# Issuing the loads of edges on ScalarE's queue in a sort-and-reduce graph kernel

## The reference

```
row = edge_index[0]                                     # src, unsorted, 400000 values below 12500
seg_sum = segment_sum(edge_attr, row, N)
seg_max = where(cnt > 0, segment_max(edge_attr, row, N), 0.0)
seg_mean = seg_sum / maximum(cnt, 1.0)
h = concatenate([seg_sum, seg_max, seg_mean, u[batch]], axis=1)
h = relu(h @ W1 + b1)
return x + (h @ W2 + b2)
```

## Time and profile before

| | us |
|---|---|
| median of 3 runs | 4303.77 (4302.16 to 4304.75) |
| the profiled execution, its own time | 4299.8 |
| its span, first to last instruction | 4298.0 |
| Pool busy | 3084.1 (72%), 3143 instructions |
| DVE busy | 2986.4 (69%) |
| PE busy | 2953.8 (69%) |
| ACT busy | 1418.7 (33%) |

### The profile page before, as it was taken

One profiled execution on the slowest core, in us unless ns is written; L12 is line 12 of the kernel. 1 busy time (PEld: TensorE's weight loads), 2 busy tenths in 40 slices (PEclk: granted clock), 3 DMA queues, 4 the chain that ended last, 5 costly groups with the idle time before them and its releaser, 6 DMA issues.

```text
span 4298.0 us, 87474 instructions
## 1 busy us (share of the span) xinstructions
PE 2953.8 (69%) x18710; PEld 2191.8 (51%) x18710; DVE 2986.4 (69%) x12043; ACT 1418.7 (33%) x4649; POOL 3084.1 (72%) x3143
## 2 busy tenths in 40 slices
PE   5677667776666666666666677777787777767747
PEld 3455446654444444444444466666665556546635
DVE  6478559974555455554455589988897888769976
ACT  3333332243333333333333323332233333322224
POOL 5777777777777777777777777776677777777620
PEclk9977558765555555555555578877776788668867
DMA  7899863311111111111111333333322333134333
GB/s 295 333 378 377 333 243 114 115 25 25 26 26 26 26 25 26 26 26 26 25 26 26 82 103 101 106 108 103 100 65 78 91 88 92 52 90 120 88 111 103
DMA packets 410044, 454.47 MB, mean 106 GB/s; under 512 B 65002, under 2 KB 381460, under 8 KB 409620
## 3 DMA queue, kind: packets, MB, share of 16 engines
q1 hardware_dynamic: 309876, 401.37, 28.4%
q0 software_dynamic: 100000, 51.40, 4.9%
HBM read 221.50 MB, written 231.02 MB: 105 GB/s over the span
## 4 chain that ended last, share of the span: by engine, by line
POOL 41%; issue 21%; DVE 20%; PE 7%; DMA 6%; POOLq 2%; DVEq 1%; ACT 1%; SPq 0%; ACTq 0%
POOL sorted_rows L439 41%; DVE peak_ps L799 5%; DMA sorted_rows<-edges,position 3%; DVE raised L782 3%; DVE picked L723 3%; PE misc_ps L526 3%; DMA edges<-in_edge_attr 2%; DVE lent L715 2%; PE start_ps L495 1%; DVE hot_owner L706 1%; POOLq L439 1%; DVE rank_c L733 1%; DVE peak_ps L777 1%; PE same_ps L472 1%; DVE raised L810 1%
## 5 line engine op out<-in xcount | busy, mean ns | idle before, releaser
L439 POOL DMA_INDIRECT sorted_rows<-edges,position x3125 | 3075.2, 984 | 1035.5 <-issue 927.7
L499 PE MATMUL place_ps<-start_sb,lent 98*128 98x128 bf16 x3125 | 877.7, 281 | 1019.2 <-DVE rank_f L723 1017.6
L610 ACT ACTIVATE start_sb<-start_ps 98x128 bf16<-98x128 f32 x3125 | 867.6, 278 | 1660.1 <-PE start_ps L495 806.0
L495 PE MATMUL start_ps<-hot_owner,hot_block 128*98 128x128 bf16 x3125 | 980.1, 314 | 143.9 <-ACT start_sb L610 105.5
L723 DVE CUSTOM_DVE_ANT_0 picked<-place_ps,hot_owner 128x128 bf16<-128x128 f32 x3125 | 886.2, 284 | 102.0 <-issue 61.5
L499 PEld LDWEIGHTS place_ps<-start_sb,lent 98*128 98x128 bf16 x3125 | 377.6, 121 | 1131.2 <-DVE rank_f L723 1100.1
L501 PE MATMUL place_ps<-hot_owner,lent 128*128 128x128 bf16 x3125 | 894.8, 286 | 0.0
L738 DVE SCALAR_TENSOR_TENSOR position<-rank_c,src_f 128x5 int32<-128x5 f32 x625 | 104.4, 167 | 1057.2 <-DMA sorted_rows<-edges,position 1007.2
L495 PEld LDWEIGHTS start_ps<-hot_owner,hot_block 128*98 128x98 bf16 x3125 | 460.6, 147 | 625.6 <-ACT start_sb L610 614.6
L472 PE MATMUL same_ps<-lent 98*128 98x128 bf16 x3125 | 654.2, 288 | 74.9 <-DVE lent L715 35.3
L526 PE MATMUL misc_ps<-win,ident_f 128*128 128x224 f32 x2548 | 699.6, 437 | 0.0
(11 more groups left out here) (79 smaller groups left out, 1402.3 us busy)
## 6 DMA issues: line engine op xcount, KB each, us to landing
sorted_rows<-zeros SPq DMA_DIRECT2D x110, 1568.0 KB, 17.1
win<-sorted_rows SPq DMA_DIRECT2D x56, 1344.0 KB
edges<-in_edge_attr SPq DMA_DIRECT2D x625, 80.0 KB
sorted_rows<-edges,position POOLq DMA_INDIRECT x3125
win<-sorted_rows SPq DMA_DIRECT2D x28, 1008.0 KB
win<-sorted_rows SPq DMA_DIRECT2D x14, 1680.0 KB
win<-sorted_rows SPq DMA_DIRECT2D x14, 1568.0 KB
win<-sorted_rows SPq DMA_DIRECT2D x14, 896.0 KB
```

Of the source, the lines that this page charges most:

```text
L439: nc.gpsimd.indirect_dma_start(out=rows[:, :], out_offset=bass.IndirectOffsetOnAxis(ap=position[:, t:t + 1], axis=0), in_=edges[:, k, j * ...
L495: nc.tensor.matmul(start_ps[0:BLOCKS, 0:P], hot_block[:, t, :], hot_owner[:, t, :], start=False, stop=False, skip_group_check=True).then_i ...
L499: nc.tensor.matmul(place_slot(j), hot_block_t[:, slot, j * P:(j + 1) * P], start_sb[:, j, :], start=True, stop=False)
L610: nc.scalar.activation(start_sb[:, j, :], start_ps[0:BLOCKS, 0:P], ACT.Copy)\
```

## The change

SP keeps its wait for the sent group but issues no load; in the load's place it increments a semaphore for which nobody waits. ACT issues the load at the end of the step in which it has copied the counts of the same group, behind the second copy of the transposed blocks. Ahead of the load ACT waits for the same `edges_sent` as SP and DVE, except for the first five groups.

```diff
--- before.py
+++ after.py
@@ -309,10 +309,6 @@
                 sp.dma_start(rows[bass.ds(plane * PLANE, PLANE), :].rearrange("(p k b) f -> p k (b f)", p=P, k=2),
                              zeros[:, :].unsqueeze(1).to_broadcast([P, 2, FILL])).then_inc(done, 16)
 
-            def load_group(c, at, k):
-                sp.dma_start(edges[:, k, :], edge_view[:, bass.ds((at * CHUNK + k * GROUP) * FEAT, GROUP * FEAT)])\
-                    .then_inc(edges_loaded[k], 16)
-
             def load_half(s, f, r, h):
                 plane = BASE[s] + r
                 part = rows[plane * PLANE:(plane + depth[s]) * PLANE, :]
@@ -348,7 +344,7 @@
                     for k in range(GROUPS):
                         if n != 0:
                             sp.wait_ge(edges_sent[k], c * (16 * GROUP))
-                        load_group(c, at, k)
+                        sp.sem_inc(pass_seen, 1)
                         if done is not None:
                             fill(at * FILLS + (BASE[1] - FILLS + k), done)
                             if k == GROUPS - 1:
@@ -622,6 +618,16 @@
                     if has(n, LAG_TRANSPOSE):
                         nc.scalar.activation(hot_block_t[:, slot, 2 * P:], hot_t_ps[0:BLOCKS, 2 * P:GROUP * P], ACT.Copy)\
                             .then_inc(hot_copied, 1)
+                    if has(n, LAG_PLACE):
+                        k = (g - LAG_PLACE) % GROUPS
+                        load_group(c - 1 if g < LAG_PLACE else c, at - 1 if g < LAG_PLACE else at, k,
+                                   n is not None and n < LAG_PLACE + GROUPS)
+
+                def load_group(c, at, k, begin):
+                    if not begin:
+                        act.wait_ge(edges_sent[k], c * (16 * GROUP))
+                    act.dma_start(edges[:, k, :], edge_view[:, bass.ds((at * CHUNK + k * GROUP) * FEAT, GROUP * FEAT)])\
+                        .then_inc(edges_loaded[k], 16)
 
                 def chunk(c, at, n, s, pair):
                     for g in range(GROUPS):
```

## The result

| | before | after |
|---|---|---|
| median of the timed runs, us | 4303.68 (4300.32 to 4311.19) | 4314.36 (4307.51 to 4325.16) |
| ratio to before, 95% interval | | 1.0026 (1.0015 to 1.0037) |
| profiled execution, its own time, us | 4299.8 | 4312.7 |
| its span, us | 4298.0 | 4311.0 |

The change makes the kernel slower by about 0.26%, some 11 us; the profiled pair stands 13.0 us apart.

The account below looks back on a forecast made before the run. Pool's scatters and their spacing were taken as the floor, 6.39 us per group of five. Start 0, wait 0, issue 4.3 and late load 0.6 summed to 4.9 us, on 4303.8 giving 4308.7 us; range 4299 to 4324.

Parts of the forecast that it names:

- likeliest case: Whole kernel: a change within 0.2%, 8.6 us, not told from no change; chance 0.62.
- The start: First loads on ACT while the zeros still run: put at 0 us, with 0.5 either way.
- The wait: ACT's wait for the sent group, ahead of the next step's copies: put at 0; uncovered, 2 us in each stretch.
- the plain stretch keeps 6.39 us a group: Sign: from 1000 to 2300 us, Pool, waiting only for its spacing, keeps 6.39 us per five scatters.
- The issue on ACT: Load's issue on ACT's queue where compute sets the time: 3.0 us (first, third stretch) plus 1.3 (second), 4.3.
- The late load: Loads landing later at the three stretches' ends: 0.2 us each, 0.6 in all, up to 2.1.
- The gain: Rival: the 31.3 us Pool waits on edges in the three stretches come back, 4272 us; chance 0.09.
- ACT held at the issue: Rival: long load issues hold ACT and delay the counts' chain at 25 boundaries, 33 us, 4337 us; chance 0.15.
- The late load in full: Rival: all 2.7 us from issue to Pool show at each of three ends, 8.1 us, 4316 us; chance 0.05.

Follow-up runs that it names:

- e11: Kernel before with the table of owners in five one-tile operations in chunks without a window, one operation in chunks with a window; 4295.35 us, ratio 0.9994.
- e2: Changed kernel with the loads issued by SP again; ACT only waits where it issued the load; 4306.42 us, ratio 1.0016.
- e10: Changed kernel with the table of owners in five one-tile operations, the owners as a scalar per partition; 4342.01 us, ratio 1.0107.
- e12: Changed kernel with the table of owners in five one-tile operations in chunks without a window, one operation in chunks with a window; 4299.31 us, ratio 0.9999.
- e9: Kernel before with the table of owners in five one-tile operations, the owners as a scalar per partition; 4340.19 us, ratio 1.0104.
- e5: Changed kernel with each load cut into four DMAs of 32 partitions, so four issues on ACT's queue; 4395.56 us, ratio 1.0228.
- e1: Changed kernel with ACT issuing each group's load one step later, when its scatters have long been sent; 4321.21 us, ratio 1.0043.
- e7: Kernel before with the table of owners in two operations, three tiles behind the fourth pick and two behind the fifth; 4302.48 us, ratio 1.0014.
- e3: Changed kernel with two small memsets on DVE ahead of each table of owners; 4306.06 us, ratio 1.0015.
- e6: e2 with the table of owners compared against the int32 iota instead of the bf16 one; 4447.8 us in the profiled execution.

## Why the prediction was off

The forecast was 4308.7 us, and its likeliest case a difference too small to tell. The time came out 5.7 us above it, within the range, and the slowdown can be told from no change (1.0015 to 1.0037). That the range held was luck: it was made wide by the bounds of the issue and of the late load, and most of the time came by another way, which the sum put at 0. Step by step:

- **The start, 0.** Right: Pool's first scatter starts at 41.20 us against 41.10. At scatter 375 after is 1.5 us late, but 1.3 of that are longer scatters; Pool idles as in before.
- **The wait, 0: this is the step that failed.** Latency was its only price that I looked for, and there I was right: Pool waits for no position in the plain stretch. (That the wait would vanish by itself did not show: ACT still stands 2.65 us in a group.) The sentence "the plain stretch keeps 6.39 us a group" was wrong: the earlier trace rows against after's row gives (992.3 + 308.6) / 1012 x 5 = 6.43. The step had seen that "PE and ACT ... will stand still", and did not ask what else stands at a fixed time on DVE once they do. The rows of before held the hint: a scatter of 1.01 us among those of 0.97, under a table of owners that began 0.33 us ahead of it. Nor was 6.39 the floor: e11, without collisions there, takes (1120.2 + 350.8) / 1152 x 5 = 6.38, and is 3.4 us faster. Of the 13 us, 7.5 came to pass here (4.3 to 11.8 us late), and 2.8 more from scatter 2450 to 2875, where the scatters are longer too (a mean of 991 ns between 3206 and 3840 us, against 985).
- **The issue on ACT, 4.3.** Right in kind. At the chunk's end that answers to the earlier trace rows the next copy follows the second copy of the transposed blocks by 1.04 us (851.49 to 852.53) where it took 0.61, so 0.43 of the load's 0.6 show, and not 0.25; e2, which waits and does not issue, has 0.61 or 0.62 in such places. Six chunk ends of the first stretch have 1.04 or 1.05 and six of the third 1.06, in after, e10 and e12 alike. At 13 ends of the second stretch it is 0.69, so 0.07 where 0.1 was put. At its six loop ends, which were put at nothing, the next copy comes 3.3 to 4.6 us behind, where before has 0.53 to 0.62; DVE stands there itself, and no run separates what it costs. The whole change, clear of collisions in the plain stretch, costs 3.0 us (e10 against e9) and 4.2 (e12 against e11) in single executions, 1.8 and 4.0 in the medians, against 4.9 foretold: of that order, and no more can be said. In these executions the second stretch, put at 1.3, carries 4.4 and 5.0 us, the first and the third together 1.4 and 2.2 in place of 3.0; since the second also moves with the clock (below), the place is not settled.
- **The late load, 0.6.** Nothing measurable at the first and the third end: position to scatter 1.14 us against 1.13. The estimate of 2.7 to 3.0 us from issue to Pool is met by 2.80 and 2.81.
- **The rivals.** The gain did not come, since the ends of the stretches belong to the position as argued. ACT held at the issue fell for one issue (400 ns at most) and is seen only with four (e5). The late load in full is what e1 pays, not after.

One size stays open. In the second stretch after made up 2.5 us (11.8 to 9.3) where the pairs above lose 4.4 and 5.0; e7, which also entered it late, made up 5.2. The windows of 2740:3160 (busy us of PE, PEld, DVE, ACT, POOL, granted clock, DMA share, GB/s) for before, after, e12:

```profile
2740.00:3160.00 420.00, 322.26 (x2080) 261.17 (x2079) 374.27 (x1287) 127.72 (x422) 299.05 (x304) 0.79 0.35 103
...
2740.00:3160.00 420.00, 315.67 (x2097) 256.48 (x2096) 378.19 (x1292) 127.65 (x422) 301.84 (x306) 0.82 0.36 103
...
2740.00:3160.00 420.00, 315.39 (x2072) 255.35 (x2071) 375.13 (x1282) 126.90 (x420) 295.75 (x300) 0.81 0.36 103
```

TensorE was granted a mean of 0.82 of full speed (2.4 GHz) in after and 0.79 in before, and PE was busy 6.6 us less. e7, with the loads on SP, had 0.81 there as well, which goes with the 5.2 us that it made up. But e11 and e12 both had 0.81 too and made nothing up, so the clock alone does not explain it; no run tested it.

## What to carry to other kernels

A wait that costs no latency can still cost time, by moving its followers against another engine's work, as the table of owners against the scatters here: before calling an added wait free, ask what its engine's followers will then overlap. Where Pool's DMAs set the time, look for a duration of theirs that is not the usual one and for the DVE operation that began just ahead of it. And test a cause of this kind by moving the suspected operation: more work on DVE, in the right place, made the plain stretch faster (e3).

## What the runs showed of the hardware

- An indirect DMA of Pool, 0.97 us by itself, is held by a DVE operation on two SBUF tables that began ahead of it, and ends 0.84 to 0.86 us behind that operation's end, whether this takes 0.29, 0.49 or 0.82 us (e6, e7). An operation of 0.63 us with one of its inputs in PSUM does not hold it (before). The int32 operand, at 0.82 us, holds it just as the bf16 one does. Which of the two gives way turned on 0.04 us: in before, after and all experiments in which the table compares two SBUF tables, one that began up to 0.039 us ahead gave way itself (in after 0.56 in place of 0.49 us at most), and one that began 0.041 us or more ahead held the scatter.
- Five one-tile comparisons with a scalar per partition took 0.90 us where one operation on the five tiles took 0.49 us. They are not free of it: 33 of the 3125 scatters were held, by 0.08 us at most (e9).
- A DMA issue took 333 to 400 ns on ACT's queue, 344 in the median, when it came once a group, also while the zeros were written (after); four of them took 1.76 us together, and up to 1.72 us each while the zeros were written (e5).
